# Routing of the tokens moved from a stage of its own into the attention, and the splitting of the experts' weights into the projection

## Time and profile before

| | us |
|---|---|
| median of 3 runs | 4200.65 |
| the profiled execution's own time | 4229.14 |
| its span, first to last instruction | 4227.2 |
| convolution | 0 to 1112 |
| projection | 1112 to 1390.3 |
| attention | 1390.3 to 3217.1 |
| routing | 3217.1 to 3638.7 |
| experts and sum | 3638.7 to 4227.2 |

### The profile page before, as it was taken

The page is one execution under the profiler, slowest core; times in us unless marked ns, Lnnn a source line. Parts: engine busy times, 40 slices in busy tenths (PEclk is TensorE's granted clock), DMA queues, the critical chain, the costliest instruction groups (busy, mean ns, idle before and its releaser), DMA issues. The chain is left out here.

```text
span 4227.2 us, 74057 instructions
## 1 busy us (share of the span) xinstructions
PE 3296.6 (78%) x26644; PEld 2558.9 (61%) x26644; DVE 2937.8 (69%) x5398; ACT 2246.0 (53%) x3488; POOL 641.4 (15%) x613
## 2 busy tenths in 40 slices
PE   5888889889466588888888888888886453599993
PEld 3656656566355467666666666666675443478782
DVE  7899999997444477777777777777775433477773
ACT  2454544544344366666666666666663221377770
POOL 1000000000010000000000000000002776466660
PEclk9999999999777799999999999999997555799995
DMA  1213213223255899999999999999994331477767
GB/s 65 78 65 120 109 71 116 88 93 112 83 209 205 289 366 362 356 369 362 382 361 370 357 361 356 351 369 355 371 366 158 121 127 44 145 236 239 238 212 318
DMA packets 281138, 988.60 MB, mean 234 GB/s; under 512 B 47796, under 2 KB 53824, under 8 KB 271734
## 3 DMA queue, kind: packets, MB, share of 16 engines
q1 hardware_dynamic: 263542, 950.62, 62.5%
q0 software_dynamic: 17280, 33.87, 2.3%
HBM read 494.69 MB, written 489.85 MB: 233 GB/s over the span
## 5 line engine op out<-in xcount | busy, mean ns | idle before, releaser
L1141 ACT ACTIVATE att_skewed<-att_skewed,att_neg_max 128x1024 f32<-128x1024 f32 x512 | 588.7, 1150 | 455.1 <-DVE att_neg_max L1201 455.0
L1272 PE MATMUL att_turn_ps<-att_ident,att_skewed 128*128 128x128 f32 x4096 | 579.9, 287 | 160.4 <-ACT att_skewed L1141 159.6
L1201 DVE CUSTOM_DVE_ANT_0 att_skewed<-att_score_ps,att_skewed 128x1024 f32<-128x1024 f32 x512 | 626.1, 1223 | 88.0 <-issue 74.0
L1272 PEld LDWEIGHTS att_turn_ps<-att_ident,att_skewed 128*128 128x128 f32 x4096 | 473.5, 146 | 346.4 <-ACT att_skewed L1141 323.8
L1132 ACT ACTIVATE att_rows<-att_wide_ps 128x1152 f32<-128x1152 f32 x512 | 572.8, 1119 | 182.6 <-PE att_wide_ps L1238 181.5
L1209 DVE COPY att_turned<-att_turn_ps 128x1024 f32<-128x1024 f32 x512 | 625.2, 1221 | 20.8 <-PE att_turn_ps L1272 20.2
L1238 PE MATMUL att_wide_ps<-att_ps,att_qs 98*128 98x128 f32 (+3 forms) x1920 | 439.8, 350 | 46.7 <-issue 25.2
L1264 PE MATMUL att_score_ps<-att_ks,att_qs 96*128 96x512 f32 x1024 | 373.3, 447 | 79.2 <-DVE att_neg_max L1201 78.3
L1238 PEld LDWEIGHTS att_wide_ps<-att_ps,att_qs 98*128 98x128 f32 x1920 | 310.2, 200 | 114.8 <-issue 66.4
L490 POOL DMA_INDIRECT expert_parts<-exp_parts,exp_rows x284 | 299.8, 1056 | 200.8 <-ACT exp_parts L521 133.7
L219 POOL DMA_INDIRECT expert_rows<-route_rows,route_place x256 | 261.2, 1020 | 104.7 <-issue 76.2
(11 more groups left out here) (257 smaller groups left out, 5670.3 us busy)
## 6 DMA issues: line engine op xcount, KB each, us to landing
skewed_rows<-att_rows SPq DMA_DIRECT2D x512, 576.0 KB, 7.6
att_skewed<-skewed_rows SPq DMA_DIRECT2D x512, 512.0 KB, 7.8
expert_rows<-conv_pad SPq DMA_DIRECT2D x144, 520.0 KB, 7.0
exp_weights<-split_weights SPq DMA_DIRECT2D x71, 1028.0 KB
att_qs<-queries SPq DMA_DIRECT2D x192, 128.0 KB, 7.8
att_ks<-keys SPq DMA_DIRECT2D x192, 128.0 KB, 6.8
exp_rows<-expert_rows SPq DMA_DIRECT2D x71, 260.0 KB
sum_part<-expert_parts SPq DMA_DIRECT2D x32, 512.0 KB, 9.4
```

The costliest lines, as they stand in the source:

```text
L1141: act.activation(skewed[r % RING][:], skewed[r % RING][:], ACT.Exp, bias=neg_max[:, k:k + 1], scale=-1.0, accum_out=sums[:, k:k + 1]).then ...
L1201: dve.tensor_tensor_reduce(skewed[r % RING][:], score_ps[:], skewed[r % RING][:], -SCALE, 3.0e38, ALU.add, ALU.min, neg_max[:, k:k + 1]).t ...
L1272: last = pe.transpose(turn_ps[:, t * P:(t + 1) * P], skewed[r % RING][:, t * P:(t + 1) * P], ident[:])
```

## The change

`route_phase` is gone. Its work is in two places.

- **Weights**: `projection_phase` stages one expert's weights at images 3 to 10, ScalarE and VectorE split them behind the image's own work, and SyncE writes them back two images later.
- **Routing**: image m is routed during the attention of image m+1, in its slots 9 to 28; image 15 in up to 28 further slots behind the last. x is taken from the attention's buffer (no load), and the load of the next x moves from slot 11 to slot 14. The PSUM space is the last 384 columns of `wide_ps`, three tiles of 128 at a time: in eight slots TensorE fills it ahead of the position scores (`fill`) and ScalarE empties it ahead of its copy to `rows` (`empty`). The moments are taken from the copy in SBUF. The normalising goes from ScalarE to GpSimd: 16 operations of 128 x 128, eight for each of the two lists, instead of eight on ScalarE and one long copy. The second turn (slots 18 to 20) waits until GpSimd has done all 16. The buffers of the routing are single where they were double or triple.

```diff
+ROUTE_AT, STATS_AT, OFFSET_AT, NORMED_AT, GATES_AT, POWER_AT, PLACES_AT, ROUTE_END = 9, 10, 15, 18, 22, 24, 25, 28
+        spare = wide_ps[:, WIDE:3 * HALF]
+        SPARE_AT = (*range(ROUTE_AT, ROUTE_AT + 3), *range(NORMED_AT, NORMED_AT + 4), PLACES_AT)
...
-            for s in range(STEPS, STEPS + ADD_LAG):
+            for s in range(STEPS, STEPS + ROUTE_END):
...
-                if s == ADD_LAG + 2 and not is_first(n) and not is_last(n):
+                if s == LOAD_X_AT and not is_first(n) and not is_last(n):
...
+            def route_rows(m):
+                pool.wait_ge(var_ready, m + 1)
+                pool.tensor_tensor(rstd[:], var[:], minus_half[:], ALU.pow).then_inc(rstd_ready, 1)
+                pool.wait_ge(offset_ready, m + 1)
+                if m:
+                    pool.wait_ge(scattered, 256 * m)
+                for k in range(2):
+                    for t in range(TT):
+                        ins = pool.tensor_scalar(expert_rows[k][:, t, 0:C], z[:, t * P:(t + 1) * P], rstd[:, t:t + 1],
+                                                 offset[:, t:t + 1], ALU.mult, ALU.add)
+                    if k == 0:
+                        ins.then_inc(normed, 1)
+                ins.then_inc(normed, 1)
+                pool.wait_ge(normed, 2 * m + 2)
+                pool.wait_ge(placed, m + 1)
+                for k in range(2):
+                    for t in range(TT):
+                        pool.indirect_dma_start(rows_dram, bass.IndirectOffsetOnAxis(ap=place[k][:, t:t + 1], axis=0),
+                                                expert_rows[k][:, t, :], None).then_inc(scattered, 16)
...
+            def empty(m, r):
+                if r - first < 3:
+                    return act.activation(z[:, cut], spare[:, 0:cut.stop - cut.start], ACT.Copy)
...
                 if s < STEPS:
                     act.wait_ge(wide_filled, STEPS * n + s + 1)
+                    if spared:
+                        empty(spared[0], spared[2])
                     at_least(act, rows_written[s % ROWS], 16 * (STEPS // ROWS * n + s // ROWS))
                     act.activation(rows[s % ROWS][:], wide_ps[:, 0:WIDE], ACT.Copy).then_inc(wide_read, 1)
...
+            def route(m, b, r):
+                if STATS_AT <= r < STATS_AT + 4:
+                    moments(m, r)
+                if r == OFFSET_AT:
+                    dve.wait_ge(rstd_ready, m + 1)
+                    dve.scalar_tensor_tensor(offset[:], mean[:], -0.5, rstd[:], ALU.mult, ALU.mult).then_inc(offset_ready, 1)
+                if GATES_AT <= r < GATES_AT + 5:
+                    gating(m, r)
...
+            def fill(m, b, r):
+                if r == ROUTE_AT:
+                    pe.wait_ge(out_added, TT * (m + 1))
+                if r == NORMED_AT:
+                    pe.wait_ge(normed, 2 * m + 2)
+                if r - first < 3:
+                    for t in range(3 * (r - first), min(3 * (r - first) + 3, TT)):
+                        last = pe.transpose(spare[:, t % 3 * P:(t % 3 + 1) * P], source, ident[:])
+                elif r == PLACES_AT:
+                    pe.wait_ge(chosen_ready, m + 1)
...
                 at_least(pe, wide_read, STEPS * n + s)
+                if spared:
+                    fill(*spared)
...
+                if 5 <= n < E + 5:
+                    keep_weights(n - 5)
+                if 3 <= n < E + 3:
+                    stage(n - 3)
...
+                if 3 <= n < E + 3:
+                    act.activation(weights_h[e % 2][:], staged[e % 2][:, 0:HALVES], ACT.Copy).then_inc(weights_high, 1)
...
+                if 3 <= n < E + 3:
+                    dve.wait_ge(weights_high, n - 2)
+                    dve.tensor_tensor(weights_l[k][:], staged[k][:, 0:HALVES], raw(weights_h[k][:]), ALU.subtract).then_inc(weights_low, 1)
...
-    route_phase(nc, NB, after_attention, expert_rows, block_table, split_weights, a["wg"], a["bg"], a["w1"], a["b1"], a["w2"],
-                a["b2"], a["ident"], a["lower"], a["before"], a["route"])
```

More of the change, by code:

```diff
@@ L975, in attention_phase @@
         marker = sb("marker", [P, 1])
+        high, low = (skewed[k][:].bitcast(F32R) for k in range(2))
+        zh, zl = (skewed[k][0:HEADS, :].bitcast(F32R) for k in range(2, 4))
+        before, ones = sb("before", [P, P]), sb("ones", [P, P])
+        lower = sb("lower", [P, E * E])
+        wgs, bgb = sb("wgs", [P, E]), sb("bgb", [P, E])
+        route_table = sb("route_table", [1, NUMBERS + BLOCKS])
+        minus_half = sb("minus_half", [P, TT])
+        token_int, token = sb("token_int", [P, TT], I32), sb("token", [P, TT])
+        positions = sb("positions", [P, (TT + 1) * E])
+        base, places = positions[:, TT * E:], positions[:, 0:TT * E].rearrange("p (t e) -> p t e", t=TT)
+        expert_rows = [sb(f"expert_rows{k}", [P, TT, ROW]) for k in range(2)]
+        place = [sb(f"place{k}", [P, TT], U32) for k in range(2)]
+        z = sb("z", [P, T])
+        stats = sb("stats", [P, 2 * TT, 3])
+        mean, apart, spread, var, rstd, offset = (sb(s, [P, TT]) for s in ("mean", "apart", "spread", "var", "rstd", "offset"))
+        product, logit, diff, power, chosen = (sb(s, [P, TT, E]) for s in ("product", "logit", "diff", "power", "chosen"))
+        second, place_one, place_two = (sb(s, [P, TT, E]) for s in ("second", "place_one", "place_two"))
+        found = sb("found", [P, 2, TT])
+        above, equal = sb("above", [P, TT, E, E]), sb("equal", [P, TT, E, E])
+        rank = sb("rank", [P, TT * E])
+        best, weight, total, gate_recip = (sb(s, [P, TT]) for s in ("best", "weight", "total", "gate_recip"))
+        count, blocks, ends = (sb(s, [1, E]) for s in ("count", "blocks", "ends"))
+        full = rows[0][0:1, 0:E * MOST_BLOCKS].rearrange("p (e k) -> p e k", e=E)
+        summed = sb("summed", [1, E, E])
+        passed, left = (rows[k][0:1, 0:BLOCKS * E].rearrange("p (k e) -> p k e", e=E) for k in range(1, 3))
+        expert, first_of, inside, begin = (sb(s, [1, BLOCKS]) for s in ("expert", "first_of", "inside", "begin"))
+        table = sb("table", [1, 2, BLOCKS], I32)
         score_ps = psum("score_ps", [P, T])
@@ L1108, in _ @@
             sp.dma_start(y_dram[NB - 1], x[1][:]).then_inc(stored, 16)
+            sp.wait_ge(placed, NB + 1)
+            sp.dma_start(table_dram, table[:].rearrange("a b c -> a (b c)")).then_inc(loaded, 16)
+            sp.wait_ge(loaded, LOADED + 16)
             sp.wait_ge(stored, 16 * NB)
+            sp.wait_ge(scattered, 256 * NB)
         @block.gpsimd
@@ L1146, in slot @@
                     act.activation(recip_t[:], tail_ps[:, P:2 * P], ACT.Copy).then_inc(recip_t_ready, 1)
+                at = routed(n, b, s)
+                if at:
+                    route(*at)
             image_loop(act, slot)
```

513 lines of the change are left out of this document (191 added, 322 removed).

## The result

The changed kernel takes 4033.85 us (median of 4 runs, 4029.83 to 4038.93) where the kernel before takes 4200.79 (4195.42 to 4201.03): a ratio of 0.9606, 95% interval 0.959 to 0.9623. That is faster, by 167 us where 260 were forecast, and inside the range of 3875 to 4050. The profiled execution took 4038.93 us, 190.2 less than the profiled one of before. First its windows by stage, to be laid beside the earlier trace rows, and then the windows of one routed image beside the earlier trace rows: projection, attention, the end of the routing (image 15), the rest; slots 0 to 11 and 12 to 31.

The account below looks back on a forecast made before the run. DMA was taken to set an attention image's time, with 9.6 us of engine room; the routing stage was a hand-over chain. 4229.1 - 421.6 + 59 + 90 + 9.8 + 2.9 = 3969.2, or 3941 against the median; range 3875 to 4050.

Parts of the forecast that it names:

- likeliest case: Whole kernel: 3941 us, 3905 to 3985 by itself, chance 0.5; attention +6 us an image, 90 us in all.
- Removed, and the end of image 15: Between attention and experts: 421.6 us of routing removed, 59 us added for image 15's routing, bounds 50 and 66.
- Projection: VectorE's weights subtraction on the path, 8 x 1.22 = 9.8 us; 18 if SyncE's cover fails, 0 if the chain has slack.
- Attention's set-up: Start of the attention: six loads of 0.44 us ahead of the vectors, 2.9 us with gaps.
- DMA, +3.2 us an image, "paid in full": Attention: the scattered rows' bytes lengthen each routed image by 3.2 us, to 113.3, since DMA is at its limit.
- 11.7 us of engine work: Each routed image: VectorE 10.0 and TensorE 6.2 us, largely in series, less 4.5 covered; 9.6 us of room.
- The stall at slot 18, "about 1 us": Attention: GpSimd's 16 normalising operations take 5.8 us in about 5 us of time, stalling TensorE about 1 us.
- Positions "half at the upper, 2.3 us", wait for `chosen` of 2 to 3 us: Slot 25: TensorE waits 2 to 3 us for VectorE, then position matmuls take 2.3 us, half their 4.6 at the lower clock.
- the hand-overs are paid in full: Rival, attention: each fill, copy, gating step and wait lengthens its slot, +9 to +13 us an image, 3985 to 4060; chance 0.22.
- GpSimd as the bound, slower: Rival, slot 18: GpSimd operations of about 1.45 us or more hold TensorE up; 4241 at the power's price; chance 0.03.
- DMA alone decides: Rival, attention: engines' additions vanish in the DMA backlog, +48 us, time 3880 to 3890; chance 0.2.
- The signs named beforehand: Expected in the profile: attention +90 us, images near 116, DMA share near 1.0, end 59, projection +10, GpSimd spacing, TensorE's waits.

Follow-up runs that it names:

- e9: Changed kernel with SyncE loading an expert's weights one image later, behind the next image's own load: 4034.4 us, 0.962 of the kernel before.
- e1: Changed kernel without the 16 indirect row transfers of each of images 0 to 14: 4001.0 us; attention's stretch 1952.4 us.
- e10: Changed kernel with offset at slot 14, position matmuls at 27, places at 28, without images 0 to 14's indirect row transfers: 3914.7 us; attention's stretch 1860.9 us.
- e5: Changed kernel with VectorE's offset made at slot 14 in place of 15, nothing else: 3990.4 us, 0.9504 of the kernel before.
- e2: Changed kernel with position matmuls at slot 27 in place of 25 and places picked at slot 28: 3966.4 us, 0.944 of the kernel before.
- e3: Changed kernel with 24 identity transposes an image added ahead of TensorE's wait for `chosen`: 3992.4 us, 0.9507 of the kernel before.
- e6: Changed kernel with offset at slot 14, position matmuls at slot 27 and places at slot 28: 3926.6 us, 0.9359 of the kernel before.
- e4: Changed kernel with GpSimd normalising only the first of the two row copies, the second left zero: 3993.8 us, 0.9497 of the kernel before.

## Why the prediction was right, and where it was off

The time lies inside the range, but the reason is in part luck. The likeliest case by itself, 3905 to 3985, does not hold 4033.9; the range does because it took in most of a rival. What the runs show as the attention's extra time, two late hand-overs with the lower clock behind them, is the reason in neither.

- **Removed, and the end of image 15**: right. 56.4 us from the last addition to the experts' first DMA for 59, with the lower clock (0.52) as expected.
- **Projection**: +11.0 for 9.8. VectorE's split on the path at 1.22 an image is confirmed (e9 has 16.33 - 15.21 = 1.12). The wait that the prediction priced as a failing cover, SyncE's landing wait ahead of the load of x, did occur (13.4 us of TensorE's waiting) but overlaps with the first cost, and so adds 2.6 us to its 9.0, not the other 8 priced for it.
- **Attention's set-up**: from its first DMA to ScalarE's first copy to `rows` 36.6 us for 33.5, +3.1 for 2.9.
- **DMA, +3.2 us an image, "paid in full"**: wrong. The scatter costs 0.9 to 1.8 us an image in the kernel as it is (e1), and with the hand-overs in time no more than about 0.6 (e10). The DMA share near 1 was taken for a limit at which each byte adds time; here it was not one. The likeliest case leaned on this twice: as its lower bound and as the reason why 11.7 us of engine work would show only as 6.
- **The stall at slot 18, "about 1 us"**: the step that was mis-sized with its clock. GpSimd's operations come 0.43 us apart where 0.36 was taken, so 6.9 us for 5.8, and TensorE was ready 4.0 us after `offset` (2331.78 to 2335.73), not 5. The wait was 3.1 us, and the price 2.9 us an image at the median (e5), not 1.
- **Positions "half at the upper, 2.3 us", wait for `chosen` of 2 to 3 us**: here the prediction failed most. The wait was 4.1 us, and the prediction counted it as part of serial work and the matmuls behind it at the upper clock. The wait itself brings the lower clock: positions 4.5 us, and the attention's matmuls behind them at half speed too. Together 4.5 us an image (e2), of which 2.8 the clock (e3). No term of the sum held this. The rows for it stood there: the old stage's chain ran at 0.53 with waits of 4.46 us before the same matmuls.
- **The rival "the hand-overs are paid in full"** gives the right time (3985 to 4060) and the right size (+10.7 us an image), but not its reason. It named the single buffers and every fill, copy and step. Two of the hand-overs hold most of the 10.7 us (e6: 107 us over 15 images is 7.2 at the median, 8.0 by the slots), and with those two in time the rest of the routing's engine work, 16.2 us an image by the prediction's count, costs 2.7 to 3.8, and up to 5.7 if the profiled execution of before is taken at its median. The forecast's expectation of cover (6 us left) was right there.
- **GpSimd as the bound, slower**: excluded by the 0.43 us.
- **The rival "DMA alone decides"** (+48 us in the attention): excluded by the +166, and by e1 and e10, where all or most of the extra time stays when the bytes are gone.
- **The signs named beforehand**: the projection and the end came out as said. GpSimd's distance (0.43 us for 0.3 to 0.4), both waits of TensorE (3.1 us for under 2, 4.1 for 2 to 3), the image (121.8 us for 116) and the DMA share (0.94 for near 1.0) did not.
- **The reference of the sum**: 23 of the 93 us between forecast and result come from carrying a profiled saving over to medians.

Left open: whether the scatter costs more beside the hand-overs than without (by the medians, less what lies in the experts' part, 1.6 and 0.4 us an image, with intervals of 8 us and more on each time); what the 1 us or so is that came back in e4 and e5 in the other slots; and what the rest at slots 25 to 28 is made of.

## What to carry to other kernels

When work moves into another loop, price each hand-over by how long TensorE stands idle before it, and price what stands behind it at the clock after that idleness. Then look for the producer's start: a slot's shift of an instruction of 0.15 us (the offset) was worth 43 us, and two slots' shift of the consumer 67. A DMA share of 0.98 did not mean here that each added byte costs its time; taking the bytes away told. Two covers that hide each other can look like next to no effect when undone one at a time, so undo both before letting a cause go.

## What the runs showed of the hardware

- GpSimd's `tensor_scalar` with two scalars per partition on 128x128 f32: 16 in 6.89 us, 0.43 us each, in the attention and in the quiet end of the routing (6.88) alike.
- Behind a wait of TensorE of 3.1 us, as behind one of 4.07, eight transposes took 1.91 us where they take 1.04 at the upper clock; with 2.84 of 4 us filled with transposes of the identity, the clock behind it was 0.82.
- The DMA engines' share was 0.98 over the attention of before; the scatter's bytes, 3.2 us of all engines an image, cost 0.9 to 1.8 us an image in one version and no more than about 0.6 in another (e1, e10).
- Adding 384 matmuls whose results nobody reads made a kernel of 4034 us 41 us faster.
